# Cross-attention of a perceiver block on one Trainium2 core: scores in three products of 64 rows, probabilities turned 64 rows at a time

## The chip, the cores and the metric

The kernel runs on one core of one Trainium2 chip. The metric is the device time of one execution in microseconds (us); the time before is the median of three executions, 1401.89 us (1398.45 to 1401.93). PE is TensorE, ACT is ScalarE, DVE is VectorE, POOL is GpSimd, SP is the queue that issues most of the DMAs. Everything is float32. A product is made of operands split in two parts, hi (rounded, type fp32r) and lo (the rest).

## The reference, cut to what matters

Three layers follow each other: cross-attention of 8 x 64 queries to 8 x 1601 context rows, a second attention with 16 heads of 64, and a mixture of experts. The change touches the first alone:

```python
x = x + xattn(layernorm(x), ctx_1024, Wq, bq, Wkv, bkv, Wproj, bproj)
# B=8 batches, N=64 queries, K=1601 context rows, D=512, H=16 heads of hd=32
q = (x @ Wq + bq)  ;  kv = (ctx @ Wkv + bkv)  ;  k, v = kv[0], kv[1]
attn = softmax(einsum('bhnd,bhkd->bhnk', q * hd**-0.5, k))
out = einsum('bhnk,bhkd->bhnd', attn, v) @ Wproj + bproj
```

## The kernel before

**Tiling.** The 1601 context rows of a batch are 13 tiles of 128 rows (the last has 65). They are worked in two chunks (`CHUNK`): chunk 0 has 7 tiles (896 keys), chunk 1 has 6 tiles (705 keys, 706 with padding). The 16 heads are 8 pairs; a pair's 2 x 64 queries fill 128 columns of `Qs_hi` and `Qs_lo`, in which the two heads stand block-diagonal, so 64 rows (2 heads x 32) carry the contraction. These 64 rows stand twice in the partitions. `Ks0` and `Ks1` hold the keys of chunk 0 and 1: the hi part in partitions 0 to 63, the lo part in 64 to 127. One matmul of 128 rows thus gives Q_hi times (K_hi + K_lo), a second one gives Q_lo times (K_hi + K_lo): four terms.

**Units and steps.** The main loop has a unit for every batch b and chunk c, 16 in all: seven batches in a hardware loop of two units each, then the last batch. A unit has nine steps (`STEPS`). Step i of a unit (functions `unit` of each engine) does on PE, in this order: `scores(i)` for pair i (L786), `turn_probs(i, 0)` and `turn_probs(i, 1)`, which transpose the probabilities of pair i-1 into two PSUM banks (L800), one or two pieces of keys or values for the chunk that comes next (`make_kv`, helper `three`, L151 to L153), a transpose of new context rows (`turn_ctx`, L694), and `outputs(i)`, the probabilities of pair i-1 times the values (L812). The last unit makes no keys or values.

**Pieces.** A chunk's keys and values come in 15 pieces (chunk 0) or 14 (chunk 1), spread over the steps of the unit before by `SLOTS`: one in step 0, two in most of the others. A key piece (K) covers four heads by 512, 384 or 322 context rows, 12 matmuls; a value piece (V) one tile of 128 rows, 12 matmuls of 512 columns. The pieces use two banks in turn: PE starts piece n when DVE is done with piece n-2 (L837); piece 5 of chunk 0 waits until pieces 0 to 4 are all done. In unit c = 1 the keys of chunk 0 are made: in steps 0 to 2 the four K pieces of 512 rows and the first V piece, in step 3 piece 5, later three K pieces and a fourth of 384 rows. In unit c = 0 the keys of chunk 1 are made, of 384 and 322 rows.

**The other engines.** In each step ACT copies the two turned banks to `PT` as hi part (`probs_hi`, L488 and L491), takes the exponential of pair i with its sum (L501), then makes the hi part of the pieces (`kv_hi`, L416 for keys, L420 for values) and of the turned context (L405). DVE takes the largest score of pair i (`largest`, L619), makes the lo part of `PT` (L628 and L632), of the pieces (`kv_lo`, L539 and L545) and of the context (L527), and adds up the output (L664). Each engine works its instructions strictly in that order. A K piece is two instructions on ACT and two on DVE, one for each pair of heads, 64 partitions each; DVE's wait for both of ACT's:

```python
ins = nc.scalar.activation(Ks[c][0:64, 2 * i + h, o:o + wide], acc[64 * h:64 * h + 64, 0:wide],
                           ACT.Identity, bias=bkc[:, 2 * i + h:2 * i + h + 1])
```

**Before the loop.** The first 15 pieces are made by themselves beside the layer norm of x and the queries (L716 to L780 on PE). `bkc`, the keys' bias, comes by one DMA of 2 KB in 4-byte elements.

**Later.** The second attention (from 1000 us) makes its scores in `score_banks` (L1494) with three products of 64 rows, two heads in turn, one in partitions 0 to 63 and one in 64 to 127, each in a PSUM bank of its own. The change leaves it as it is.

Of the kernel before, what the change touches and what calls it, by code (L numbers as in the profile page):

```python
# [24 lines left out]
def perceiver_kernel(nc, x_in, ctx_in, Wq, bq, Wkv, bkv, Wproj, bproj,  # L25
# [3 lines left out]
    P = 128  # L29
# [15 lines left out]
    HALF = [2 * -(-w // 4) for w in WIDE]  # L45
# [18 lines left out]
    with ExitStack() as whole:  # L64
# [107 lines left out]
        Ks0 = late("Ks0", [P, NP, WIDE[0]], FR)  # L172
# [19 lines left out]
        Ks1 = early("Ks1", [P, NP, WIDE[1]], FR)  # L192
# [11 lines left out]
        bkc = early("bkc", [64, NP])  # L204
# [3 lines left out]
        part_s = early("part_s", [P, BE, 2, NP])  # L208
        whole_s = early("whole_s", [P, BE, NP])
        factor = early("factor", [P, 2 * NP * B])  # L210
        factorT = early("factorT", [P, P])
        top7 = early("top7", [P, NP])
# [55 lines left out]
        def prob_groups(c):  # L268

            return (range(0, 4), range(4, CHUNK[c][1]))  # L270
# [36 lines left out]
        def program(block):  # L307
# [32 lines left out]
            def _(sp):  # L340
# [4 lines left out]
                sp.dma_start(bkc[:, :], bkv[0:D].rearrange("(j r) -> r j", r=64), allow_slow_non_contiguous=True).then_inc(sem("bk_in"), 16)  # L345
# [18 lines left out]
                def units(b):  # L364
# [7 lines left out]
                    sp.wait_ge(sem("s_made"), pairs_before(b, 1) + 4)  # L372
# [3 lines left out]
                    sp.wait_ge(sem("s_made"), pairs_before(b, 1) + NP)  # L376
# [24 lines left out]
            def _(act):  # L401
# [6 lines left out]
                def kv_hi(n, acc, c, piece):  # L408
                    kind, s, i = piece_of(c, piece)
                    t0, _ = SUBS[c][s]  # L410
                    o = (t0 - CHUNK[c][0]) * P
                    act.wait_ge(sem("kv_made"), n + 1)
                    if kind == "K":
                        _, wide = sub_cols(c, s)
# [23 lines left out]
                act.wait_ge(sem("bk_in"), 16)  # L438
# [39 lines left out]
                def unit(b, c, turn0, ctx, beside=None):  # L478
# [3 lines left out]
                    def probs_hi(i, q):  # L482
                        n = turn_of_probs(i, q, ctx)
                        acc = bank(P_BANKS[q])
                        tiles = prob_groups(c)[q]
                        full = [t for t in tiles if tile_rows(CHUNK[c][0] + t) == P]
                        act.wait_ge(sem("turned"), turn0 + n + 1)
                        ins = nc.scalar.copy(PT[:, full[0]:full[-1] + 1, 0, :],  # L488
                                             acc[:, 0:P * len(full)].rearrange("p (t r) -> p t r", r=P))
                        if len(full) < len(tiles):  # L490
                            ins = nc.scalar.copy(PT[0:TAIL, tiles[-1], 0, :],  # L491
                                                 acc[0:TAIL, P * len(full):P * len(tiles)])
                        ins.then_inc(sem("turn_hi"), 1)
# [29 lines left out]
            def _(dve):  # L523
# [6 lines left out]
                def kv_lo(n, acc, c, piece):  # L530
                    kind, s, i = piece_of(c, piece)
                    t0, _ = SUBS[c][s]
                    o = (t0 - CHUNK[c][0]) * P
                    dve.wait_ge(sem("kv_hi"), n + 1)
                    if kind == "K":
                        _, wide = sub_cols(c, s)
                        for h in range(2):
                            j = 2 * i + h
                            ins = nc.vector.scalar_tensor_tensor(  # L539
                                out=Ks[c][64:128, j, o:o + wide], in0=acc[64 * h:64 * h + 64, 0:wide],  # L540
                                scalar=bkc[:, j:j + 1], in1=f32(Ks[c][0:64, j, o:o + wide]),
                                op0=ALU.add, op1=ALU.subtract)
# [22 lines left out]
                dve.wait_ge(sem("bk_in"), 16)  # L565
# [47 lines left out]
                def unit(b, c, turn0, ctx, beside=None, begin=None, between=None):  # L613
# [3 lines left out]
                    def largest(i):  # L617
                        dve.wait_ge(sem("s_made"), pair0 + i + 1)
# [3 lines left out]
                    def probs_lo(i, q):  # L622
                        n = turn_of_probs(i, q, ctx)
                        acc = bank(P_BANKS[q])
                        tiles = prob_groups(c)[q]
# [1578 lines left out]
```

## Time and profile before

| | us |
|---|---|
| median of 3 runs | 1401.89 |
| the profiled execution, its own time | 1393.57 |
| its span in the profile | 1391.8 |
| before the main loop | 0 to 69 |
| a unit c = 0 (step 0 to step 0) | 182.4 to 238.4 |
| a unit c = 1 | 238.4 to 296.6 |
| the last unit | about 922 to 955 |
| seam, second attention, experts | 955 to the end |

The profile has a page (busy time of each engine, the chain of work that ended last, costliest groups of instructions) and views of the trace: who waited for whom, the timeline, groups by form, and busy time in chosen stretches. A duration given for a PE instruction contains its way through the engine and overlaps with the next; the distance between two starts is what it costs. In a timeline neighbours of one form are merged ("x7"); a row has the start, the length of the merged stretch, the engine, the line, the operation, and tiles written and read; forms are rows*columns of the stationary block, then rows x columns of what is streamed. PEld is the load of the stationary block.

### The profile page before, as it was taken

How to read it: one execution, taken by the hardware profiler on the slowest of the kernel's cores; microseconds unless marked ns; L12 is line 12 of the kernel's file. 1: busy time of each engine (PE TensorE's matmuls, PEld its weight loads, DVE VectorE, ACT ScalarE, POOL GpSimd, SP SyncE). 2: the span in 40 equal slices, each digit the busy share in tenths (PEclk: the TensorE clock that was granted, in tenths of full speed). 3: DMA queues.
4: the chain of work that ended last, by engine and by line, in shares of the span. 5: the costliest groups of instructions: out<-in, count | busy, mean ns of one | idle time of the engine just before them, and what ended most of it. 6: DMA issues, size and time to landing. Idle time of an engine off the chain costs nothing.

```text
span 1391.8 us, 22065 instructions
## 1 busy us (share of the span) xinstructions
PE 1325.6 (95%) x7439; PEld 1149.9 (83%) x7440; DVE 937.9 (67%) x1512; ACT 760.0 (55%) x1327; POOL 101.6 (7%) x84
## 2 busy tenths in 40 slices
PE   7999999999999999999999999987899699999997
PEld 5898988888889898888889989976677587877776
DVE  6566666666667666666666766758488856487884
ACT  5465555565555555555556554654332526477772
POOL 0000000000000000000000000044452120000002
PEclk9999999999999999999999999999899899999999
DMA  5211121011111112101111010472538457399993
GB/s 196 95 54 32 30 52 43 26 45 35 44 30 38 30 34 60 30 26 45 45 34 45 23 39 27 82 156 71 94 112 307 149 197 255 112 349 333 342 346 106
DMA packets 126852, 145.11 MB, mean 104 GB/s; under 512 B 64072, under 2 KB 67528, under 8 KB 126800
## 3 DMA queue, kind: packets, MB, share of 16 engines
q1 hardware_dynamic: 125536, 140.44, 32.6%
q0 software_dynamic: 1280, 4.20, 0.9%
q8 instruction: 22, 0.36, 0.1%
q14 instruction: 14, 0.11, 0.0%
HBM read 124.75 MB, written 19.86 MB: 104 GB/s over the span
## 4 chain that ended last, share of the span: by engine, by line
PE 71%; DVE 13%; issue 6%; DMA 4%; ACT 4%; SPq 1%; DVEq 0%; POOL 0%; ACTq 0%
PE ps_scores L151 12%; PE ps_scores L153 12%; PE ps_scores L152 12%; PE ps_out L819 6%; PE ps_turn L807 5%; PE ps_scores L796 5%; PE ps_turn L694 2%; DMA wu_raw<-in_L_ffn_W_dram 2%; PE ps_scores L2116 2%; PE ps_scores L2114 2%; PE ps_scores L2115 2%; DVE stat L619 2%; DVE Ks L539 2%; ACT wu_hi L1823 1%; DVE wu_lo L2005 1%
## 5 line engine op out<-in xcount | busy, mean ns | idle before, releaser
L539 DVE SCALAR_TENSOR_TENSOR Ks<-ps_scores,bkc,Ks 64x384 fp32r<-64x384 f32 (+2 forms) x254 | 160.6, 632 | 143.4 <-ACT Ks L416 140.8
L151 PE MATMUL ps_scores<-cT_hi,Wkv_hi 128*128 128x384 f32 (+2 forms) x504 | 181.9, 361 | 0.0
L501 ACT ACTIVATE Pr<-ps_scores,stat 128x705 f32<-128x705 f32 (+1 forms) x128 | 119.5, 934 | 110.0 <-DVE stat L619 110.0
L153 PE MATMUL ps_scores<-cT_hi,Wkv_lo 128*128 128x384 f32 (+2 forms) x504 | 172.9, 343 | 0.0
L152 PE MATMUL ps_scores<-cT_lo,Wkv_hi 128*128 128x384 f32 (+2 forms) x504 | 172.4, 342 | 0.0
L416 ACT ACTIVATE Ks<-ps_scores,bkc 64x384 fp32r<-64x384 f32 (+2 forms) x254 | 149.4, 588 | 39.1 <-PE ps_scores L153 35.5
L545 DVE TENSOR_TENSOR Vs<-ps_scores,Vs 128x512 fp32r<-128x512 f32 (+1 forms) x103 | 71.2, 691 | 147.0 <-ACT Vs L420 146.4
L151 PE MATMUL ps_scores<-Wkv_hi,cT_hi 128*128 128x512 f32 (+1 forms) x412 | 169.9, 412 | 0.0
L488 ACT CAST PT<-ps_turn 128x512 fp32r<-128x512 f32 (+2 forms) x256 | 110.2, 483 | 102.4 <-PE ps_turn L807 101.5
L153 PE MATMUL ps_scores<-Wkv_hi,cT_lo 128*128 128x512 f32 (+1 forms) x412 | 161.8, 393 | 0.0
L152 PE MATMUL ps_scores<-Wkv_lo,cT_hi 128*128 128x512 f32 (+1 forms) x412 | 161.1, 391 | 0.0
L819 PE MATMUL ps_out<-PT,Vs 128*128 128x256 f32 x832 | 123.2, 286 | 16.2 <-DVE PT L632 11.9
L2005 DVE TENSOR_TENSOR wu_lo<-wu_raw,wu_hi 128x2048 fp32r<-128x2048 f32 x56 | 126.5, 2287 | 15.8 <-ACT wu_hi L1823 15.7
L628 DVE TENSOR_TENSOR PT<-ps_turn,PT 128x512 fp32r<-128x512 f32 (+2 forms) x256 | 130.0, 550 | 10.3 <-ACT PT L488 9.4
L819 PEld LDWEIGHTS ps_out<-PT,Vs 128*128 128x128 f32 x832 | 113.6, 189 | 27.6 <-DVE PT L632 15.5
L420 ACT CAST Vs<-ps_scores 128x512 fp32r<-128x512 f32 (+1 forms) x103 | 60.4, 586 | 138.0 <-PE ps_scores L153 137.1
L619 DVE TENSOR_REDUCE stat<-ps_scores 128x1 f32<-128x705 f32 (+1 forms) x128 | 125.7, 983 | 3.4 <-DVE stats L670 3.3
L1823 ACT CAST wu_hi<-wu_raw 128x2048 fp32r<-128x2048 f32 x56 | 105.8, 1917 | 21.0 <-DMA wu_raw<-in_L_ffn_W_dram 21.0
L807 PE MATMUL ps_turn<-ident,Pr 128*128 128x128 f32 x832 | 112.7, 274 | 0.0
L807 PEld LDWEIGHTS ps_turn<-ident,Pr 128*128 128x128 f32 x832 | 98.5, 141 | 5.8
L153 PEld LDWEIGHTS ps_scores<-cT_hi,Wkv_lo 128*128 128x128 f32 x504 | 94.7, 188 | 5.2
L152 PEld LDWEIGHTS ps_scores<-cT_lo,Wkv_hi 128*128 128x128 f32 x504 | 95.1, 189 | 4.0
(383 smaller groups left out, 2466.8 us busy)
## 6 DMA issues: line engine op xcount, KB each, us to landing
wu_raw<-in_L_ffn_W_dram SPq DMA_DIRECT2D x64, 1024.0 KB, 7.4
raw<-in_ctx_dram SPq DMA_DIRECT2D x16, 768.0 KB, 4.6
raw<-in_ctx_dram SPq DMA_DIRECT2D x8, 1024.0 KB, 5.4
raw<-in_ctx_dram SPq DMA_DIRECT2D x8, 512.0 KB
sorted_x<-zeros SPq DMA_DIRECT2D x1, 4096.0 KB, 14.9
sorted_out<-zeros SPq DMA_DIRECT2D x1, 4096.0 KB, 25.4
o_heads<-U SPq DMA_DIRECT2D x56, 64.0 KB, 1.7
oA<-o_heads SPq DMA_DIRECT2D x8, 448.0 KB, 9.4
```

The costliest lines, as they stand in the source:

```text
L151: nc.tensor.matmul(out_ap, sh, mh, start=(i == 0), stop=False)
L152: nc.tensor.matmul(out_ap, sh, ml, start=False, stop=False)
L153: last = nc.tensor.matmul(out_ap, sl, mh, start=False, stop=(i == len(pairs) - 1))
L416: ins = nc.scalar.activation(Ks[c][0:64, 2 * i + h, o:o + wide], acc[64 * h:64 * h + 64, 0:wide], ACT.Identity, bias=bkc[:, 2 * i + h:2 * ...
L501: nc.scalar.activation(Pr[:, i % 2, 0:VALID[c]], S_cols(c, 0, VALID[c], 0 if ctx else i % 2), ACT.Exp, bias=stat[:, 0, c, i:i + 1], accum_ ...
L539: ins = nc.vector.scalar_tensor_tensor(out=Ks[c][64:128, j, o:o + wide], in0=acc[64 * h:64 * h + 64, 0:wide], scalar=bkc[:, j:j + 1], in1= ...
L619: nc.vector.tensor_reduce(stat[:, 0, c, i:i + 1], S_cols(c, 0, VALID[c], 0 if ctx else i % 2), AX.X, ALU.max, negate=True).then_inc(sem("s ...
L628: ins = nc.vector.tensor_tensor(PT[:, full[0]:full[-1] + 1, 1, :], acc[:, 0:P * len(full)].rearrange("p (t r) -> p t r", r=P), f32(PT[:, f ...
L807: ins = nc.tensor.matmul(bank(P_BANKS[q])[0:M, at:at + P], Pr[:, (i - 1) % 2, t * P:t * P + M], ident[:, :], is_transpose=True, start=True ...
L819: ins = nc.tensor.matmul(psO_heads, Vs[c][0:M, t, i - 1, :], PT[0:M, t, :, :].rearrange("p a r -> p (a r)"), start=(t == 0), stop=(t == CH ...
L1823: nc.scalar.copy(wu_hi[v][:, :, :], wu_raw[v % RING][:, :, :]).then_inc(sem("wu_hi_done"), 1)
L2005: nc.vector.tensor_tensor(wu_lo[v][:, :, :], wu_raw[v % RING][:, :, :], f32(wu_hi[v][:, :, :]), ALU.subtract).then_inc(sem("wu_lo_done"), 1)
```

## The change

The scores become the three products Q_hi K_hi, Q_hi K_lo and Q_lo K_hi of 64 rows each. The keys of a chunk are cut in two halves (`HALF`: 448 and 448 in chunk 0, 384 and 322 in chunk 1). The first half stands, hi and lo, in partitions 0 to 63, the second in 64 to 127; `Ks` keeps its size. The six matmuls alternate between the two halves of the partitions and between two PSUM banks. A K piece of 512 rows (context rows 0 to 511 of chunk 0) straddles the cut at 448, so ACT and DVE each write it with four instructions (2 x 448 and 2 x 64 columns) in place of two; all other K pieces lie in one half. `bkc` is needed in both halves and comes by two DMAs. The probabilities are turned one head at a time: for each tile two transposes of 64 rows and 64 streamed columns, head 0 into one bank and head 1 into the other; both banks are told of after the last tile. ACT and DVE each copy two banks of 64 columns by 7 or 6 tiles, where chunk 1 had three instructions. The wait for the banks moves ahead of the scores. Some small buffers share memory.

```diff
-    HALF = [2 * -(-w // 4) for w in WIDE]
+    HALF = [448, 3 * P]
...
-        Ks0 = late("Ks0", [P, NP, WIDE[0]], FR)
+        Ks0 = late("Ks0", [P, NP, 2, HALF[0]], FR)
...
+        def key_halves(c, s):
+            o, wide = (SUBS[c][s][0] - CHUNK[c][0]) * P, sub_cols(c, s)[1]
+            found = []
+            for half, (h0, h1) in enumerate(((0, HALF[c]), (HALF[c], WIDE[c]))):
+                k0, k1 = max(o, h0), min(o + wide, h1)
+                if k0 < k1:
+                    found.append((half, slice(k0 - o, k1 - o), slice(k0 - h0, k1 - h0)))
+            return found
+        def turned_probs(c, h):
+            n = CHUNK[c][1]
+            return bank(P_BANKS[h])[:, 0:S * n].rearrange("p (t r) -> p t r", r=S)
+        def kept_probs(c, h, part):
+            return PT[:, 0:CHUNK[c][1], part, S * h:S * (h + 1)]
...
-                sp.dma_start(bkc[:, :], bkv[0:D].rearrange("(j r) -> r j", r=64), ...)
+                for half in range(2):
+                    sp.dma_start(bkc[64 * half:64 * half + 64, :], bkv[0:D].rearrange("(j r) -> r j", r=64), ...)
...
# kv_hi on ACT; kv_lo on DVE is cut in the same way
-                        for h in range(2):
-                            ins = nc.scalar.activation(Ks[c][0:64, 2 * i + h, o:o + wide], acc[64 * h:64 * h + 64, 0:wide],
-                                                       ACT.Identity, bias=bkc[:, 2 * i + h:2 * i + h + 1])
+                        for half, cols, to in key_halves(c, s):
+                            rows = slice(64 * half, 64 * half + 64)
+                            for h in range(2):
+                                j = 2 * i + h
+                                ins = nc.scalar.activation(Ks[c][rows, j, 0, to], acc[64 * h:64 * h + 64, cols],
+                                                           ACT.Identity, bias=bkc[rows, j:j + 1])
...
# probs_hi on ACT; probs_lo on DVE in the same way
-                        ins = nc.scalar.copy(PT[:, full[0]:full[-1] + 1, 0, :], ...)
-                        if len(full) < len(tiles):
-                            ins = nc.scalar.copy(PT[0:TAIL, tiles[-1], 0, :], ...)
-                        ins.then_inc(sem("turn_hi"), 1)
+                        nc.scalar.copy(kept_probs(c, q, 0), turned_probs(c, q)).then_inc(sem("turn_hi"), 1)
...
# scores on PE
-                        for part, Q in enumerate((Qs_hi, Qs_lo)):
-                            for k0, k1 in ((0, HALF[c]), (HALF[c], WIDE[c])):
-                                ins = nc.tensor.matmul(S_cols(c, k0, k1, 0 if ctx else i % 2), Q[:, i, :],
-                                                       Ks[c][:, i, k0:k1], start=(part == 0), stop=(part == 1))
-                        ins.then_inc(sem("s_made"), 1)
+                        if ctx and i >= 1:
+                            pe.wait_ge(sem("turn_lo"), turn0 + turns_free(i))
+                        for n, (part, Q) in enumerate(((0, Qs_hi), (1, Qs_hi), (0, Qs_lo))):
+                            for half, (k0, k1) in enumerate(((0, HALF[c]), (HALF[c], WIDE[c]))):
+                                rows = slice(64 * half, 64 * half + 64)
+                                ins = nc.tensor.matmul(S_cols(c, k0, k1, 0 if ctx else i % 2), Q[rows, i, :],
+                                                       Ks[c][rows, i, part, 0:k1 - k0], start=(n == 0), stop=(n == 2))
+                                if n == 2:
+                                    ins.then_inc(sem("s_made"), 1)
...
# turn_probs on PE
-                            ins = nc.tensor.matmul(bank(P_BANKS[q])[0:M, at:at + P],
-                                                   Pr[:, (i - 1) % 2, t * P:t * P + M], ident[:, :],
-                                                   is_transpose=True, start=True, stop=True)
-                        ins.then_inc(sem("turned"), 1)
+                            for h in range(2):
+                                rows = slice(64 * h, 64 * h + 64)
+                                ins = nc.tensor.matmul(bank(P_BANKS[h])[0:M, S * t:S * (t + 1)],
+                                                       Pr[rows, (i - 1) % 2, t * P:t * P + M], ident[rows, rows],
+                                                       is_transpose=True, start=True, stop=True)
+                                if t == last:
+                                    ins.then_inc(sem("turned"), 1)
```

## Rows read from the trace of the kernel before

**Rows 1.** The page: busy time of PE; engines' shares of the last chain.
```profile
PE 1325.6 (95%) x7439; PEld 1149.9 (83%) x7440; DVE 937.9 (67%) x1512; ACT 760.0 (55%) x1327; POOL 101.6 (7%) x84
PE 71%; DVE 13%; issue 6%; DMA 4%; ACT 4%; SPq 1%; DVEq 0%; POOL 0%; ACTq 0%
```

**Rows 2.** Busy time by stretch: one unit c = 0, one unit c = 1.
```profile
182.40:238.40 56.00, 54.91 (x342) 49.74 (x341) 37.89 (x64) 33.24 (x64) 0.00 (x0) 1.00 0.18 52
238.40:296.60 58.20, 57.88 (x334) 51.53 (x333) 37.34 (x71) 31.68 (x71) 0.00 (x0) 1.00 0.10 25
```

**Rows 3.** Who waited for whom, 68 to 922: us, times, longest; PE's own waits.
```profile
PEld ps_scores L796 <- ACT Pr L501: 5.6, 7, 0.9
PEld ps_out L819 <- DVE PT L628: 5.3, 8, 0.8
```

**Rows 4.** Timeline of PE, one step of a unit c = 0, then c = 1.
```profile
307.67 0.57 PE L796 MATMUL ps_scores<-Ks,Qs_hi 128*128 128x448 f32 x2
...
308.49 0.93 PE L807 MATMUL ps_turn<-ident,Pr 128*128 128x128 f32 x7
309.17 0.42 PE L151 MATMUL ps_scores<-cT_hi,Wkv_hi 128*128 128x384 f32 x1
309.43 0.33 PE L152 MATMUL ps_scores<-cT_lo,Wkv_hi 128*128 128x384 f32 x1
...
364.21 0.49 PE L796 MATMUL ps_scores<-Ks,Qs_hi 128*128 128x354 f32 x2
...
364.87 0.82 PE L807 MATMUL ps_turn<-ident,Pr 128*128 128x128 f32 x6
```

**Rows 5.** Timeline of PE, second attention: into and out of its 64-row scores.
```profile
1005.51 0.39 PE L153 MATMUL ps_scores<-x2T_hi,sW_lo 128*128 128x512 f32 x1
1005.83 0.39 PE L1494 MATMUL ps_turn<-QT_hi,KT_hi 64*128 64x256 f32 x2
1006.05 0.28 PE L1494 MATMUL ps_turn<-QT_lo,KT_hi 64*128 64x256 f32 x2
1006.16 0.28 PE L1494 MATMUL ps_turn<-QT_hi,KT_lo 64*128 64x256 f32 x2
...
1012.91 0.31 PE L1494 MATMUL ps_scores<-QT_hi,KT_lo 64*128 64x256 f32 x2
1013.15 0.50 PE L151 MATMUL ps_turn<-x2T_hi,sW_hi 128*128 128x512 f32 x1
1013.48 0.39 PE L152 MATMUL ps_turn<-x2T_lo,sW_hi 128*128 128x512 f32 x1
```

**Rows 6.** Timeline, four float32 transposes of 8 rows and 8 streamed columns.
```profile
1105.99 0.32 PEld L2074 LDWEIGHTS ps_turn<-ident,lgT 8*128 8x128 f32 x4 [1.02 <-ACT lgT L1801]
1105.99 0.41 PE L2074 MATMUL ps_turn<-ident,lgT 8*128 8x8 f32 x4 [0.83 <-ACT lgT L1801]
```

**Rows 7.** Groups by form, 68 to 922: the keys' hi and lo parts.
```profile
L539 DVE SCALAR_TENSOR_TENSOR Ks<-ps_scores,bkc,Ks 64x384 fp32r<-64x384 f32 x120 | 73.9, 616 | 66.8 <-ACT Ks L416 65.6
L416 ACT ACTIVATE Ks<-ps_scores,bkc 64x384 fp32r<-64x384 f32 x120 | 69.0, 575 | 13.3 <-PE ps_scores L153 12.5
L539 DVE SCALAR_TENSOR_TENSOR Ks<-ps_scores,bkc,Ks 64x512 fp32r<-64x512 f32 x56 | 42.0, 749 | 42.6 <-ACT Ks L416 42.2
L416 ACT ACTIVATE Ks<-ps_scores,bkc 64x512 fp32r<-64x512 f32 x56 | 38.2, 682 | 9.3 <-PE ps_scores L153 9.0
```

**Rows 8.** Timeline, a unit c = 1: pieces 3 and 4 leave, piece 5 starts.
```profile
370.16 1.51 DVE L539 SCALAR_TENSOR_TENSOR Ks<-ps_scores,bkc,Ks 64x512 fp32r<-64x512 f32 x2 [1.29 <-ACT Ks L416]
...
372.19 0.69 DVE L545 TENSOR_TENSOR Vs<-ps_scores,Vs 128x512 fp32r<-128x512 f32 x1
...
373.32 0.47 PE L151 MATMUL ps_scores<-Wkv_hi,cT_hi 128*128 128x512 f32 x1
```

**Rows 9.** Timeline: x turned before the loop; the outputs of the last unit.
```profile
30.88 1.10 PE L735 MATMUL ps_turn<-ident,x_tok 128*128 128x128 f32 x8 [2.91 <-DVE x_tok L137]
...
939.86 0.39 PE L819 MATMUL ps_out<-PT,Vs 128*128 128x256 f32 x1 [0.93 <-DVE PT L632]
```

More of the change, by code:

```diff
@@ L191, in perceiver_kernel @@
         early = area(EARLY, LATE)
-        Ks1 = early("Ks1", [P, NP, WIDE[1]], FR)
+        Ks1 = early("Ks1", [P, NP, 2, HALF[1]], FR)
         Vs1 = early("Vs1", [P, CHUNK[1][1], NP, P], FR)
@@ L203, in perceiver_kernel @@
                 early("rt1", [P, TT]), early("rs1", [P, TT]))
-        bkc = early("bkc", [64, NP])
+        bkc = early("bkc", [P, NP])
         bqc = early("bqc", [P, KC])
@@ L207, in perceiver_kernel @@
         part_f = early("part_f", [P, BE, 2, NP])
[L208 to L209 removed]
+        whole_s = top
         factor = early("factor", [P, 2 * NP * B])
         factorT = early("factorT", [P, P])
+        part_s = factorT[:, 0:BE * 2 * NP].rearrange("p (b c j) -> p b c j", b=BE, c=2)
         top7 = early("top7", [P, NP])
@@ L344, in _ @@
                     sp.dma_start(Wkv_raw[:, k, :], wkv[:, k, :]).then_inc(sem(f"wkv_in{k}"), 16)
-                sp.dma_start(bkc[:, :], bkv[0:D].rearrange("(j r) -> r j", r=64), allow_slow_non_contiguous=True).then_inc(sem("bk_in"), 16)
+                for half in range(2):
+                    sp.dma_start(bkc[64 * half:64 * half + 64, :], bkv[0:D].rearrange("(j r) -> r j", r=64),
+                                 allow_slow_non_contiguous=True).then_inc(sem("bk_in"), 16)
                 sp.dma_start(x_tok[:, :, :], x_rows).then_inc(sem("x_in"), 16)
@@ L532, in kv_lo @@
                     t0, _ = SUBS[c][s]
-                    o = (t0 - CHUNK[c][0]) * P
                     dve.wait_ge(sem("kv_hi"), n + 1)
                     if kind == "K":
[L536 to L542, printed above, removed]
+                        for half, cols, to in key_halves(c, s):
+                            rows = slice(64 * half, 64 * half + 64)
+                            for h in range(2):
+                                j = 2 * i + h
+                                ins = nc.vector.scalar_tensor_tensor(
+                                    out=Ks[c][rows, j, 1, to], in0=acc[64 * h:64 * h + 64, cols],
+                                    scalar=bkc[rows, j:j + 1], in1=f32(Ks[c][rows, j, 0, to]),
+                                    op0=ALU.add, op1=ALU.subtract)
                     else:
@@ new lines, in turns_free, with turn_probs @@
+                    def turns_free(i):
+                        return 0 if i == 1 else turn_of_probs(i - 1, 1, ctx) + 1
+                    def turn_probs(i):
+                        if not ctx or i == NP:
+                            pe.wait_ge(sem("p_exp"), pair0 + i + 1)
+                            pe.wait_ge(sem("turn_lo"), turn0 + turns_free(i))
+                            pe.sem_inc(sem("turn_begun"), 1)
+                        last = CHUNK[c][1] - 1
+                        for t in range(last + 1):
+                            M = tile_rows(CHUNK[c][0] + t)
+                            for h in range(2):
+                                rows = slice(64 * h, 64 * h + 64)
[4 more added lines that the diff above has]
+                                    ins.then_inc(sem("turned"), 1)
```

44 lines of the change are left out of this document (9 added, 35 removed).

## The prediction

> **What bounds the kernel now.** I read the page first: PE is busy for 95% of the span and makes 71% of the chain that ended last; DVE at 67% and ACT at 55% have room on the average [rows 1]. The change lies almost wholly in the main loop, so next the busy time by stretch: in a unit c = 0 PE is busy 54.9 of 56.0 us, in a unit c = 1 57.9 of 58.2 [rows 2]. Then the list of waits over the loop: PE's own are 5.6 us for the exponential and 5.3 us for the turned probabilities in 854 us, some 0.7 us in 7 and 8 places [rows 3]. So PE's stream of starts sets the loop, and a tenth of a microsecond in a step counts 120 times (8 steps, 15 units). But DVE's averages hide one tight place, which the timeline shows: in a unit c = 1 the value piece 5 starts on PE at 373.32, and what it waits for, piece 4 on DVE, ends at 372.19 + 0.69 = 372.88 [rows 8]. That is 0.44 us of slack, with DVE having stood idle for 1.29 us before piece 3 only because ACT was not done with it. Last, the second attention, since it already has pairs of 64-row products [rows 5].
>
> **The scores.** Before: four matmuls of 448 columns from 307.67 to 308.49, 0.82 us or 0.205 each; in c = 1 364.21 to 364.87, 0.66 us, 0.164 each [rows 4]. Do two 64-row matmuls on different halves run side by side? In the second attention each merged row is two of them ("x2"), and pairs of 256 columns start 0.11 to 0.12 us apart, 1006.05 to 1006.16 [rows 5]: two for what one of 256 columns costs by the slope of the rows above (0.205 to 0.164 for 94 columns, so about 0.12). They do. So the scores take three pair times: 3 x 0.205 = 0.615 in c = 0 (saves 0.205); in c = 1 the wider half decides, 384 columns, at the pitch of a 384-column matmul, 0.174 (0.164 for 354, and the same slope), 3 x 0.174 = 0.52 (saves 0.13).
>
> **The turns.** Before: seven transposes; to the second key matmul after them it is 308.49 to 309.43, and in steady state one takes 0.109 (0.68 for 6 of them and 0.03 of the last, whose rest hides behind the next load) [rows 4]. What binds one, its load or its 128 streamed columns? Four small transposes of the experts' routing have the same kind of transpose with the same 128-column block and only 8 streamed columns: four loads in 0.32 us, one of 0.136 and three pitches of 0.06; four transposes in 0.41, pitches near 0.065 [rows 6]. So the load costs 0.06 and it is the stream that takes 0.109, 0.85 ns a column. With 64 columns in each half side by side the stream needs 0.055 and the load 0.06: I take 0.062 for a pair. Seven pairs: 0.43 for 0.76, saves 0.33; six: saves 0.28. Bounds: 0.055 (the stream alone) and 0.124 (the two loads one after the other). ACT and DVE get both banks 0.43 us after the first transpose where they got the first bank after 4 x 0.109 = 0.44: nothing moves for them. Their copies cost the same in c = 0 and under 0.1 us less in c = 1 (three instructions become two).
>
> **Going in and out.** The pieces and the outputs stay at 128 rows, so each step goes from 128 to 64 rows and back. Into them: L153 starts at 1005.51 and lasts 0.23 (512 columns at 0.44 ns and the overhead in the rows of L796), so 1005.74 would be next; it is 1005.83, and the second pair comes 0.22 later instead of 0.12 [rows 5]. Together 0.19: the engine runs empty first, then the first load (0.11) stands bare. Out: the last pair starts at 1012.91, without a change the second matmul of 512 columns would be at 1012.91 + 0.12 + 0.23 = 1013.26, it is 1013.48: 0.22 [rows 5]. After a transpose a part of this is paid already (the first key matmul lasts 309.17 to 309.43, 0.26 for 0.17 [rows 4]), the pair is shorter, and I come to 0.20. The list of places is the same in all 15 units with pieces: 9 steps, each in and out. Bounds 0.15 and 0.23 a way; nothing below, since both crossings in rows 5 pay.
>
> The Trainium skill says the same of this ("TensorEngine Tiling (Array Packing)", Key Properties: changing the tiling mode drains the engine) and gives no price; the trace's price is the one used. A rule that speaks against the narrow transposes is in "TensorE: Matmul & The Clock Gate", LDWEIGHTS: a load takes its columns / 1.2 ns, so 107 ns for 128 columns however few rows. For the fp32r loads of rows 5 this holds (0.11); for the float32 transposes of rows 6 it does not (0.06). By it the turns would gain nothing; that result is the second rival.
>
> **Sum on PE.** A step in c = 0: +0.19 - 0.205 - 0.33 + 0.20 = -0.15. In c = 1: +0.19 - 0.13 - 0.28 + 0.20 = -0.02. A unit c = 0 has six such steps that count (1 to 5 and 7). Step 0 (scores alone) ends in the wait for the exponential and step 6 (one piece) in the one for the turned probabilities [rows 3]: both chains start at the scores, which come as early as before (+0.19 - 0.205), so nothing is won there. Step 8 (turns alone): in, with a cheap load, +0.15, -0.33, +0.20, zero. Unit: -0.9. The added wait ahead of the scores is for what outputs(i-1) had already waited for: nothing.
>
> **The keys' copies.** A K piece of 512 rows gets four instructions on each engine. ACT: 682 and 575 ns for 512 and 384 columns [rows 7] is 0.84 ns a column, so 629 for 448 and, as an estimate, 308 for 64: +0.255 a head pair, +0.51 a piece. DVE: 749 and 616, 1.04 a column, 682 and 284: +0.43. DVE waits for ACT, so 0.94 us in series. (Bounds: nothing, if 64 columns cost what 64 more cost; 0.94 is from a line through three widths down to 322.) Unit c = 1 has four such pieces ahead of piece 5. I follow the two queues through steps 1 to 3. Piece 0: +0.94 on DVE. Behind it stands the largest score of step 1, which ACT's exponential waits for, and behind that piece 1 on ACT: +1.9 when DVE is done with it. Piece 2's ACT part runs in ACT's free time: +2.0. Then largest, exponential, piece 3: +2.9, and piece 4 behind it: +2.9 at 372.88. With 0.44 of slack, piece 5 starts 2.45 late, whatever PE saved until then. Behind it come value pieces (one instruction each), and the queues recover. Step 0's crossings (+0.19 - 0.13 + 0.19) put piece 0 itself some 0.2 later, and steps 4 to 8 come out even (four of -0.02, and step 8 with +0.15 - 0.28 + 0.20): +2.6 a unit. This is why I expect a loss: seven units c = 1, and the four long pieces are all of the same chunk.
>
> **Before the loop.** The same pieces 0 to 3 stand in DVE's queue ahead of the layer norm, and PE stands 2.91 us idle for x at 30.88 [rows 9]. Going through the queues as above, pieces 0 to 2 bring +1.3 and piece 3, inside the norm, +0.43: +1.75. The second DMA for `bkc` takes SP some 0.7 us more and delays x_tok by as much; the wait in rows 9 is for DVE and not for that DMA, so it is hidden. **Last unit:** it is a chain of outputs, turns, ACT, DVE (PE waits 0.93 for DVE [rows 9]); ACT's and DVE's shorter copies bring about 0.1 a step: -0.7.
>
> **Total.** 8 x (-0.9) + 7 x 2.6 + 1.75 - 0.7 = -7.2 + 18.2 + 1.05 = +12. The profiled execution took 1393.57 (its span 1391.8 and 1.8 around it), so 1405.6 there; the runs shown have a median 8.3 above it, and I move the median by the same 12: 1414.
>
> **Rivals.**
> First, the other side: the copies' extra instructions stay hidden. Place: piece 5 in c = 1; it decides at 0.44 us of added delay, against my 2.9. For it: 0.94 a piece rests on a line extended to 64 columns, and DVE is idle a third of the unit (37.3 busy of 58.2 [rows 2]). Against: the idle time stands where DVE waits for ACT, in the very series that grows. Then -7.2, units c = 1 about +0.2 each (step 0's +0.25 and the rest from above), -0.7 and little before the loop: -7, 1395; with crossings of 0.15, 1389. Chance 0.18.
> Second, the loads bind the turns: a pair takes 0.109 or more, as for an fp32r block. For: 64-row float32 loads on two halves are nowhere in the trace. Against: rows 6, and fp32r loads do pair in rows 5. Then 0.047 x 7 x 8 x 8 = +21 in c = 0; in c = 1 only steps 4 to 8 count, 0.047 x 6 x 5 x 7 = +10; the waits of rows 3 take up some 6. 1414 + 25 = 1439. Chance 0.16.
> Third, the halves do not run side by side with blocks of this kind: scores +0.6, turns +0.3 a step: some +90, 1500. Rows 5 speak against it; 0.02.
> Fourth, all my costs at their low ends together (crossings 0.15, the 64-column instructions half as dear): -6 and -9, near 1399 to 1405, no change. Chance 0.12.
>
> **Chances and range.** Forecast 0.52, so slower 0.52 + 0.16 + 0.02 = 0.70, within 0.3% (1397.7 to 1406.1, about what a measurement tells from no change) 0.12, faster 0.18. The forecast's own range is 1406 to 1428 (pair time 0.055 to 0.08, crossings to 0.23). To hold eight in ten it goes from the first rival's 1396 to the second's 1440.
>
> **What would show it.** Rows of L796's successor "x2" at 0.205 apart: scores in pairs. Starts of the transposes' pairs 0.06 apart, or 0.11 for the second rival. 0.19 and 0.20 more at the crossings. The group of the keys' lo part with a 64x64 form near 284 ns, ACT's near 308. A new wait of PE for DVE's value piece 4, some 2 us in each unit c = 1, which then lasts near 60.8 us, and units c = 0 near 55. If no such wait shows, the forecast is wrong and the first rival right.

## The result: 2.6% slower, where 0.9% was forecast

The changed kernel takes 1435.62 us (median, 1433.36 to 1437.84), the kernel before 1400.17 beside it: ratio 1.026, 95% interval 1.024 to 1.028. The forecast was 1414 with a range of 1396 to 1440. The sign and the range hold, but the loss is 35 us and not 12. The profiled execution took 1435.29, its span 1433.5.

The page of the kernel after, as [rows 1], and its line of instruction packets:
```profile
PE 1331.7 (93%) x8527; PEld 1121.7 (78%) x8528; DVE 949.0 (66%) x1512; ACT 777.1 (54%) x1327; POOL 101.6 (7%) x84
q8 instruction: 78, 1.28, 0.4%
PE 60%; DVE 17%; issue 10%; ACT 7%; DMA 5%; SPq 1%; POOL 0%; DVEq 0%; ACTq 0%
```
The same line of packets on the page of before:
```profile
q8 instruction: 22, 0.36, 0.1%
```
PE is busy only 6 us more, in a span 42 us longer. What grew are "issue" (6 to 10% of the last chain), ACT and DVE on that chain, and the instruction packets, 22 to 78. None of my terms was about the last. The share of "issue" misleads here: e1 below, without the gaps that follow, has 10% as well.

Busy time by stretch, after, as [rows 2]: the first unit c = 0, a unit c = 1, the unit c = 0 behind it (columns: stretch, length, PE, PEld, DVE, ACT and POOL busy, granted clock, DMA share, GB/s):
```profile
73.90:128.60 54.70, 53.76 (x414) 46.91 (x414) 37.30 (x62) 33.61 (x64) 0.00 (x0) 1.00 0.17 50
248.40:311.90 63.50, 58.38 (x397) 49.70 (x396) 39.69 (x74) 34.94 (x72) 0.00 (x0) 1.00 0.10 24
312.00:368.20 56.20, 55.26 (x414) 48.11 (x414) 36.71 (x61) 32.03 (x62) 0.00 (x0) 0.97 0.18 52
```
From start of scores to start of scores the units c = 1 take 63.2 to 63.6 us (before 58.2; one 64.9, the last 61.3), the units c = 0 54.8 (before 55.9), but four of them 56.3. The loop starts at 73.9 (before 68.9) and its last unit at 960.5 (before 921.7). From there to the end it is 2.9 us more. So 5.0 before the loop, 33.8 in it, 2.9 behind: 41.7, the difference of the spans. It is above that of the medians, 35.4, since the profiled execution of before (1393.57) lay 6.6 us under its median. The 2.9 behind can't be told from chance: kernels that leave that part as it is (before, e2, e8 to e11) need 470 to 478 us for it, after 473.

PE's own waits in the loop, after, as [rows 3] (us in total, times, longest):
```profile
PE ps_scores L151 <- DVE Vs L554: 12.5, 7, 1.8
PE ps_scores L799 <- issue: 12.1, 6, 2.2
PE ps_out L832 <- DVE PT L634: 11.5, 16, 1.0
PE ps_scores L151 <- DVE Ks L548: 3.3, 7, 0.5
```
Seven waits of 1.8 us are the forecast wait for value piece 4, one in each unit c = 1. The six waits for "issue" ahead of the scores, 2.2 us each, were not forecast. They stand where PE's loop over the batches turns. The timeline of PE there, between the last two units above:
```profile
308.88 0.87 PE L832 MATMUL ps_out<-PT,Vs 128*128 128x256 f32 x6
311.95 1.11 PE L799 MATMUL ps_scores<-Ks,Qs_hi 64*128 64x448 f32 x4 [2.20 <-issue]
312.86 0.58 PE L799 MATMUL ps_scores<-Ks,Qs_lo 64*128 64x448 f32 x2
313.37 0.69 PE L151 MATMUL ps_scores<-cT_hi,Wkv_hi 128*128 128x384 f32 x1
```
PE stands for 2.2 us with nothing to wait for, and when it starts again the clock is down. Two stretches from there:
```profile
311.80:315.20 3.40, 3.25 (x12) 2.67 (x13) 1.09 (x1) 0.57 (x1) 0.00 (x0) 0.50 0.50 86
315.20:318.60 3.40, 3.40 (x34) 3.09 (x33) 0.79 (x2) 2.50 (x7) 0.00 (x0) 1.00 0.80 302
```
The granted clock is 0.50 (1.2 GHz) in the first and 1.00 in the second, and 12 matmuls run in the first where 34 run in the second. So a gap can cost twice: its 2.2 us, and 1.5 us of half clock right behind it. The four units c = 0 of 56.3 us are these. The unit c = 1 of 64.9 has its half clock (509.7 to 513.1) not behind a gap but at the end of the wait for value piece 4 (509.8).

### The profile page after: what moved, and what is told of

Its sections match the earlier page's. It is cut to its first block, busy times and chain, and to the rows that moved or that the text cites. A ratio compares the mean times of both kernels' runs of the same rounds, so it can differ in the third digit from the quotient of the medians.

```text
span 1433.5 us, 24234 instructions
## 1 busy us (share of the span) xinstructions
PE 1331.7 (93%) x8527; PEld 1121.7 (78%) x8528; DVE 949.0 (66%) x1512; ACT 777.1 (54%) x1327; POOL 101.6 (7%) x84
## 4 chain that ended last, share of the span: by engine, by line
PE 60%; DVE 17%; issue 10%; ACT 7%; DMA 5%; SPq 1%; POOL 0%; DVEq 0%; ACTq 0%
PE ps_scores L151 12%; PE ps_scores L153 10%; PE ps_scores L152 10%; PE ps_out L832 5%; PE ps_scores L799 4%; ACT Ks L433 4%; DVE Ks L548 3%; PE ps_turn L819 2%; DVE stat L628 2%; DMA b1rows<-b_parts 2%; PE ps_turn L694 2%; DVE wu_lo L2017 2%; PE ps_scores L2128 2%; PE ps_scores L2126 2%; PE ps_scores L2127 2%
## 5 line engine op out<-in xcount | busy, mean ns | idle before, releaser
L548 DVE SCALAR_TENSOR_TENSOR Ks<-ps_scores,bkc,Ks 64x384 fp32r<-64x384 f32 (+3 forms) x316 | 174.3, 552 | 161.7 <-ACT Ks L433 158.3
L151 PE MATMUL ps_scores<-cT_hi,Wkv_hi 128*128 128x384 f32 (+2 forms) x504 | 186.8, 371 | 3.3 <-DVE Ks L548 3.3
L433 ACT ACTIVATE Ks<-ps_scores,bkc 64x384 fp32r<-64x384 f32 (+3 forms) x316 | 165.3, 523 | 41.5 <-PE ps_scores L153 35.0
L502 ACT CAST PT<-ps_turn 128x448 fp32r<-128x448 f32 (+1 forms) x256 | 117.2, 510 | 89.7 <-PE ps_turn L819 89.3
L634 DVE TENSOR_TENSOR PT<-ps_turn,PT 128x448 fp32r<-128x448 f32 (+1 forms) x256 | 138.6, 583 | 12.1 <-ACT PT L502 10.1
L1835 ACT CAST wu_hi<-wu_raw 128x2048 fp32r<-128x2048 f32 x56 | 105.8, 1917 | 18.2 <-DMA wu_raw<-in_L_ffn_W_dram 16.4
L151 PEld LDWEIGHTS ps_scores<-cT_hi,Wkv_hi 128*128 128x128 f32 x504 | 96.3, 191 | 16.5 <-DVE Ks L548 4.2
L151 PEld LDWEIGHTS ps_scores<-Wkv_hi,cT_hi 128*128 128x128 f32 (+1 forms) x412 | 76.6, 186 | 31.7 <-DVE Vs L554 13.5
```

Of the source, the lines that this page charges most:

```text
L151: nc.tensor.matmul(out_ap, sh, mh, start=(i == 0), stop=False)
L433: ins = nc.scalar.activation(Ks[c][rows, j, 0, to], acc[64 * h:64 * h + 64, cols], ACT.Identity, bias=bkc[rows, j:j + 1])
L502: nc.scalar.copy(kept_probs(c, q, 0), turned_probs(c, q)).then_inc(sem("turn_hi"), 1)
L548: ins = nc.vector.scalar_tensor_tensor(out=Ks[c][rows, j, 1, to], in0=acc[64 * h:64 * h + 64, cols], scalar=bkc[rows, j:j + 1], in1=f32(Ks ...
L634: nc.vector.tensor_tensor(kept_probs(c, q, 1), turned_probs(c, q), f32(kept_probs(c, q, 0)), ALU.subtract).then_inc(sem("turn_lo"), 1)
L1835: nc.scalar.copy(wu_hi[v][:, :, :], wu_raw[v % RING][:, :, :]).then_inc(sem("wu_hi_done"), 1)
```

## The parts of the change measured by their own rows

Timeline of PE, one step of a unit c = 0, after, as [rows 4]:
```profile
83.78 0.28 PE L832 MATMUL ps_out<-PT,Vs 128*128 128x256 f32 x1
83.99 0.67 PE L799 MATMUL ps_scores<-Ks,Qs_hi 64*128 64x448 f32 x4
84.50 0.36 PE L799 MATMUL ps_scores<-Ks,Qs_lo 64*128 64x448 f32 x2
84.70 0.59 PE L819 MATMUL ps_turn<-ident,Pr 64*128 64x64 f32 x14
85.22 0.44 PE L151 MATMUL ps_scores<-cT_hi,Wkv_hi 128*128 128x384 f32 x1
85.50 0.34 PE L152 MATMUL ps_scores<-cT_lo,Wkv_hi 128*128 128x384 f32 x1
```
The last score pair takes 84.50 to 84.70, 0.20 (forecast 0.205). The two before it take 0.51, so the first has 0.10 too much, and 83.78 to 83.99 is 0.21 where an output matmul's pitch is 0.12: into 64 rows costs 0.19 (forecast 0.19). Fourteen transposes and the way out take 0.52: six pitches of 0.061 (forecast 0.062) and 0.15; the rest of the way out is in the first key matmul, 85.22 to 85.50, 0.28 for 0.26 before. From the first score to the second key matmul it is 1.51 us and 0.09 of late arrival, before 1.76 [rows 4]: a step is 0.16 shorter, and 0.15 was forecast.

The keys' copies in the loop, after, as [rows 7]:
```profile
L548 DVE SCALAR_TENSOR_TENSOR Ks<-ps_scores,bkc,Ks 64x448 fp32r<-64x448 f32 x56 | 38.1, 680 | 53.8 <-ACT Ks L433 53.4
L433 ACT ACTIVATE Ks<-ps_scores,bkc 64x448 fp32r<-64x448 f32 x56 | 35.2, 629 | 7.9 <-PE ps_scores L153 7.4
L433 ACT ACTIVATE Ks<-ps_scores,bkc 64x64 fp32r<-64x64 f32 x56 | 17.2, 308 | 0.7
L548 DVE SCALAR_TENSOR_TENSOR Ks<-ps_scores,bkc,Ks 64x64 fp32r<-64x64 f32 x56 | 16.0, 286 | 0.8
```
629, 308, 680 and 286 ns: forecast 629, 308, 682 and 284. The line through three widths held down to 64 columns.

Timeline in a unit c = 1, after, as [rows 8]: pieces 3 and 4 leave, piece 5 starts:
```profile
268.83 1.98 DVE L548 SCALAR_TENSOR_TENSOR Ks<-ps_scores,bkc,Ks 64x448 fp32r<-64x448 f32 x4 [1.76 <-ACT Ks L433]
...
271.31 0.68 DVE L554 TENSOR_TENSOR Vs<-ps_scores,Vs 128x512 fp32r<-128x512 f32 x1
...
272.05 0.50 PE L151 MATMUL ps_scores<-Wkv_hi,cT_hi 128*128 128x512 f32 x1 [1.77 <-DVE Vs L554]
```
PE starts piece 5 as soon as DVE is done with piece 4, and has stood 1.77 us for it.

## Experiments: the loop's turn

Theory: the loop's body outgrew PE's instruction memory. One turn has 1467 recorded instructions before (672 matmuls, as many loads, 123 of the sequencer) and 1738 after (808, 808, 122). The expectations below name some bodies by sums that come out a few higher (1744, 1757, 1675, 1670, 1699, 1728); outside them the text gives what the traces hold. The records are not quite whole: of e2's 290 added instructions three a turn have none.

**e1: after with PE's loop written out.**
```
-                with pe.Fori(0, BE) as b:
+                for b in range(BE):
```


> The changed kernel with PE's loop over the batches written out (the other engines keep theirs). Theory A, the loop's turn: PE's loop body grew from 1467 to 1744 recorded instructions and no longer stays in its instruction store, so that at each of six turns PE stands 2.2 to 2.5 us for instructions and its clock then halves for 3.4 us in most of them. Written out, the body is fetched in a straight line: the gap before the scores of a new batch goes, 6 x 2.3 plus about 5 x 1.5 of half clock, so about 1435.6 - 21 = 1414, near the forecast. Rival B, the gap is the tail of the copies' longer queues on ACT and DVE: nothing changes there, 1432 to 1437. Rival C, that fetching itself costs more than is thought, in or out of a loop: slower than 1436.

1424.58 us (1422.28 to 1428.61), ratio to before 1.019 (1.017 to 1.022). The gaps are gone, with no wait of PE for "issue" left in the loop; units c = 0 take 55.3, units c = 1 61.3, but two of them 62.8. The turn was 11.0 of the 35.4 us. The rest is 10.6 us above my 1414. Its waits, and the half clock in one of the two longer units:
```profile
PE ps_scores L151 <- DVE Vs L554: 12.7, 7, 1.8
PE ps_out L832 <- DVE PT L634: 10.2, 15, 0.9
PE ps_scores L151 <- DVE Ks L548: 3.3, 7, 0.5
385.30:388.80 3.50, 3.50 (x11) 2.57 (x10) 1.05 (x3) 0.94 (x2) 0.00 (x0) 0.52 0.20 42
```
It stands 1 us behind the end of a 1.8 us wait for value piece 4, with no gap near: here too the copies' wait was followed by half clock, in two units of seven.

**e2: before with 290 semaphore increments more in a turn** (nobody waits for that semaphore; a body of 1754).
```
             for i, ((sh, sl), (mh, ml)) in enumerate(pairs):
+                for _ in range(pads[0] + (pads[1] if i == 0 else 0)):
+                    pe.sem_inc(sem("pad"), 1)
...
+                pads[:] = [2, 2]
                 with pe.Fori(0, BE) as b:
...
+                pads[:] = [0, 0]
```


> The kernel before, with 290 more PE instructions per turn of its loop, all increments of an unused semaphore among the key and value products (10 a piece, 29 pieces): a body of about 1757 with the old arithmetic. Theory A: instruction fetches go on through the loop (the kernel before has none between 188 and 891 us), a gap of 2.2 to 2.5 us at each of six turns and half clock behind it, 1400 + 14 to 22 = 1414 to 1422. Rival B (queues of the copies) and rival C' (the 64-row products bring the gap): no gap, 1400 to 1403, unless the increments themselves show between the matmuls.

1410.56 us (1408.98 to 1412.70), ratio 1.0085 (1.0064 to 1.0105), under the 1414 I expected at least. The gap is there at each turn, in a kernel with nothing of the change:
```profile
PE ps_scores L800 <- issue: 12.5, 6, 2.2
PE ps_out L823 <- DVE PT L632: 3.3, 8, 0.5
```
There are 77 instruction packets, and two units c = 0 of 56.7 and 56.8 us, half clock again. The others behind a gap last 55.3 where before has 55.9: ACT and DVE catch up while PE stands, which gives 0.6 us back (PE's seven waits for the exponential, 4.3 us in before, become one of 0.4). The unit of 56.8 by stretch:
```profile
186.40:243.20 56.80, 56.40 (x341) 51.35 (x342) 36.79 (x61) 31.98 (x62) 0.00 (x0) 0.97 0.17 51
```

**e8: before with its loop written out**, the control for e1 and e4.

> Before with TensorE's loop written out and nothing else changed, the control for the written-out loops. Theory A (the loop of before costs nothing at its turn, since its body stays in the instruction memory, and straight-line fetch costs nothing): 1399 to 1401, unit lengths as before, but as many instruction packets as the written-out after has. Rival (writing the loop out wins time of its own, so that what e1 and e4 gained was not the change's loss taken back): 1390 to 1396.

1398.94 us (1396.80 to 1401.42), ratio 0.9996 (0.9984 to 1.0008): a tie. It reads 54 packets and its units last 55.9 and 58.2 as before. So reading instructions in a straight line costs nothing that shows. What costs is the turn of a long body, with its packets.

**e9, e10, e11: where the bound lies.** As e2, with other counts:
```
-                pads[:] = [2, 2]
+                pads[:] = [1, 3]
```
This is e9 against e2; e10 has [2, 0] there, e11 [2, 1].

> Before with 203 always-granted semaphore increments among TensorE's key and value products of a turn (e2 had 290): a body of about 1670 recorded instructions, as e6's 1675. Theory A (the instruction memory holds a body up to a bound between 1675 and 1744, whatever the instructions are): no gap at the turn of the loop, unit lengths of before, about 22 instruction packets, 1399 to 1403. Rival (increments and matmuls count differently, or the place of the branch decides): gaps of 2.2 to 2.5 us at each turn, 1408 to 1413.

> The same with 232 increments, a body of about 1699: one look for the bound. A bound in the middle of 1675 and 1744 leaves open whether the gap is there; with it a turn takes 2.0 to 2.5 us more and about 77 instruction packets are read, without it about 22.

> The same with 261 increments, a body of about 1728: one look for the bound. With a bound near 1710, where seven blocks of 256 instructions less what the body wastes at its ends would lie, the gap is there.

e9, a body of 1667: 1399.57 us, ratio 1.001 (0.998 to 1.004), no gap, 23 packets, though one of its ten runs took 1413.83. e10, 1696: 1413.76, with a gap at four of the six turns. e11, 1725: 1415.47, a gap at all six. e10 and e11 ran once each. Two turns in e10, one with and one without the gap:
```profile
416.53 0.88 PE L823 MATMUL ps_out<-PT,Vs 128*128 128x256 f32 x6
420.03 0.68 PE L800 MATMUL ps_scores<-Ks,Qs_hi 128*128 128x448 f32 x2 [2.63 <-issue]
...
534.25 0.88 PE L823 MATMUL ps_out<-PT,Vs 128*128 128x256 f32 x6
534.96 0.58 PE L800 MATMUL ps_scores<-Ks,Qs_hi 128*128 128x448 f32 x2
```
So the bound is near 1700 recorded instructions and not sharp: in one and the same execution a body of 1696 turns with the gap and without it. Between 100 and 880 us the instruction packets are 5 in e9 (no gap), 41 in e10 (four gaps) and 59 in e11 (six): 9 for each gap.

The Trainium skill says ("Runtime: NRT & Kernel Launch", Instruction fetch mechanics) that PE's instruction memory holds 2048 instructions and is filled in blocks of 256, and that a taken branch to a target outside a window of two blocks stalls the engine until the block is fetched. The traces agree with the stall and show its price here, 2.2 to 2.6 us. They put the bound for a loop below 2048, near 1700 as far as records count. A window of two blocks they don't bear out: a body of 1467 turns without a gap. What the runs show is the stall, its packets, and that both hang on the number of instructions in the body; that a memory no longer holds the body is my reading of it, and no run counts what the memory holds.

## Experiments: the keys' copies

**e3: before with its 512-column key pieces copied as 448 and 64.**
```
-                        for h in range(2):
+                        for k0, k1 in ((0, 448), (448, 512)) if wide == 512 else ((0, wide),):
+                            for h in range(2):
...
```


> The kernel before, with only the copies of the 512-row key pieces cut at 448 columns, four instructions each on ACT and DVE. The forecast's term: 0.94 us more in series a piece, 2.45 a unit c = 1 after 0.44 of slack, 7 x 2.45 + 1.75 before the loop = +19, so 1419; a wait of PE for DVE of some 2.5 us at piece 5 in each of seven units. The forecast's first rival, copies hidden: 1400 to 1402 and no such wait.

1421.41 us (1419.66 to 1426.45), ratio 1.017 (1.014 to 1.020). The cut alone costs 21.6 us. Units c = 1 last 61.1 for 58.2, units c = 0 stay at 55.9, and the loop starts at 73.8 for 68.9. Its main wait is the one forecast for the change, 1.7 us where I said some 2.5; smaller ones for DVE, of 0.2 and 0.25 us, come ahead of it:
```profile
PE ps_scores L151 <- DVE Vs L547: 11.8, 7, 1.7
```

Before the loop the cut does more than delay. PE turns x, in before [rows 9], here in e3 and then in after, each with its stretch from 28 to 50 us:
```profile
33.26 1.97 PE L737 MATMUL ps_turn<-ident,x_tok 128*128 128x128 f32 x8 [4.26 <-DVE x_tok L137]
28.00:50.00 22.00, 17.74 (x82) 14.66 (x81) 14.95 (x29) 8.64 (x15) 0.00 (x0) 0.84 0.06 20
```
```profile
33.31 1.97 PE L735 MATMUL ps_turn<-ident,x_tok 128*128 128x128 f32 x8 [4.28 <-DVE x_tok L137]
28.00:50.00 22.00, 17.72 (x82) 14.64 (x81) 14.99 (x30) 8.64 (x15) 0.00 (x0) 0.84 0.07 19
```
The wait grew from 2.91 to 4.3 us, and behind it the granted clock is 0.84 in the mean of 22 us where before has 1.00: some 7 us at half clock, 3.5 lost. The eight transposes take 1.97 for 1.10. But the profile of before is a fortunate one. In e8, which is before up to the loop, the same stretch has
```profile
30.78 1.50 PE L735 MATMUL ps_turn<-ident,x_tok 128*128 128x128 f32 x8 [2.92 <-DVE x_tok L137]
28.00:50.00 22.00, 19.22 (x92) 16.15 (x93) 13.94 (x24) 7.53 (x15) 0.00 (x0) 0.92 0.10 30
```
a wait of the same length with a clock of 0.92 behind it, and the loop starts at 70.3. In e11 it is 0.84, again behind a wait of 2.91, and the start is 71.6. So the length of the wait alone does not set the clock, and kernels that are before up to the loop start it anywhere from 68.9 to 71.6. The second DMA for `bkc` has no part in this: e3 has only the one of before, and starts its loop as late as after.

**e4: e1 with the cut pieces copied head by head**, and DVE told after the first head, so that it copies head 0 while ACT copies head 1.
```
-                        for half, cols, to in key_halves(c, s):
-                            for h in range(2):
+                        for h in range(2):
+                            for half, cols, to in key_halves(c, s):
...
+                            if h == 0 and (c, s) == (0, 0):
+                                ins.then_inc(sem("k_part"), 1)
```


> The changed kernel with PE's loop written out and the cut key pieces copied one head after the other: ACT tells DVE after the first head (the other half of the bank's partitions), so that the series is 0.94 + 0.97 + 0.97 = 2.88 us, as in the kernel before (2.89), in place of 3.8. Theory A with the forecast's terms: the wait at piece 5 (7 x about 2) goes as well, 1414 - 7 x 2.5 - 1 = 1395 to 1398, below the kernel before. If the load of the engines and not the series made the wait, ACT and DVE still carry four instructions a piece and it stays: 1412 to 1414.

1401.49 us (1398.10 to 1405.18), ratio 1.002 (1.0004 to 1.0037), 3.5 us above the 1395 to 1398 I expected and not below before. Against e1 it is 23.1 us. The wait for piece 4 is gone, and a unit c = 1 lasts 58.4 us:
```profile
PE ps_out L843 <- DVE PT L644: 11.1, 16, 1.0
PE ps_scores L810 <- ACT Pr L512: 3.0, 7, 0.5
```
```profile
184.80:240.20 55.40, 53.93 (x413) 46.99 (x412) 37.76 (x64) 33.21 (x64) 0.00 (x0) 1.00 0.17 53
240.20:298.70 58.50, 58.05 (x399) 49.84 (x398) 38.63 (x72) 33.80 (x72) 0.00 (x0) 1.00 0.09 26
```
The instructions are all still there; only the series of ACT and DVE was cut. From the loop's start to that of the last unit it is 3.0 us shorter than before; what stands ahead of the loop is 2.7 longer.

**e12: e4 with PE's loop kept**, which completes the square of loop and copies.

> e4 with TensorE's loop kept as in after: only the order of the copies of the cut keys' pieces is changed against after. Theory A (the loop's turn and the copies are two separate losses that add up): e4's 1401.5 plus the 11.0 us that after lost against e1, 1410 to 1415; units with c=0 54.8 or 56.3 us, with c=1 60.4 to 60.7, gaps of 2.2 to 2.5 us at the turn. Rival (what is left of the copies' wait and the gap hide each other): 1403 to 1407. Other rival (the loss at the turn grows as nothing else holds TensorE): over 1418.

1410.30 us (1408.04 to 1412.83), ratio 1.008 (1.005 to 1.011). The turn costs 8.8 us here and 11.0 with the slow copies; the copies cost 23.1 with the loop written out and 25.3 with it kept. So the two losses add up, to within 2.2 us.

## Experiments: scores and turns apart, and the best version

**e5: the scores alone** (keys, scores and e4's order of copies of after, turns of before, loop kept).

> After's scores (three products of 64 rows for each half of the keys, the cut keys' pieces copied head by head with VectorE told after the first head), with the turns of before and TensorE's loop kept; its body would be about 1531 recorded instructions (before 1467, after 1744). Theory A (the score pairs save 0.15 us a step with 448 and 448 keys and less with 384, and the two crossings between whole-array and 64-row matmuls cost 0.19 and 0.20 us once a step, whoever of the two parts brings them): a unit with c=0 +1.1 us and with c=1 +1.7 us against before, 20 us in the loop, +2.7 us before it: 1417 to 1424. Where a body of 1531 no longer stays in TensorE's instruction memory (gaps of over 2 us at the turn of the loop), 10 to 14 us more: 1428 to 1437. Rival (the scores carry the whole gain of the change and the crossings are hidden): at or under 1403.

**e6: the turns alone** (before with the turns and the probabilities' copies of after).

> After's turns (64-row transposes, one head each, side by side) with the scores, the keys and their copies of before, and TensorE's loop kept; its body would be about 1675 recorded instructions. Theory A (the pairs of transposes save about what the two crossings cost): +0.02 us a step with c=0, +0.07 with c=1: 1402 to 1407 if the body stays in the instruction memory, and with gaps of over 2 us at the turn of the loop 1412 to 1421. Rival (the turns alone win and the scores lose): under 1397. If e5 (1531) has no gap and this one (1675) has, the bound lies between them.

e5: 1419.85 us (1417.42 to 1420.47), ratio 1.014 (1.012 to 1.016), as expected, without a gap and with 22 packets. Units c = 0 last 56.8 and c = 1 59.8, against 55.9 and 58.2. e6: 1405.92 us (1400.86 to 1417.51), ratio 1.006 (1.003 to 1.008); its profiled run took 1400.86, units of 56.0 and 58.5, no gap. Each part alone pays the crossings and loses, e6 2.7 of its 5.5 us by the longer units of its profiled run. Together they pay once and, as e4 shows, gain 0.6 us in a unit c = 0. e6 and e9, with bodies of 1674 and 1667, scatter by 17 and 18 us where e4 with ten runs too has 7. That a gap comes in some of their executions would explain it; neither profile is of such a run, so it is not shown.

**e7: e4 with the low part of key piece 3 behind the layer norm.**
```
-                norm_vector(dve, 1, x_tok, x_tok, lnt1, between=lambda: first_kv_lo(3))
+                norm_vector(dve, 1, x_tok, x_tok, lnt1)
+                first_kv_lo(3)
```


> e4 (after, TensorE's loop written out, cut keys' pieces copied head by head) with the low part of the fourth keys' piece behind the normalisation on VectorE and not in the middle of it. In the trace of e4 that copy (1.97 us) stands between the variance and the reciprocal, whose root is there at 27.36 us, and TensorE waits 4.3 us for x_tok. Theory: TensorE's wait falls to about 2.6 us but some of it comes back at the next product of values, which needs that copy: loop start 71.6 to between 70.5 and 71.2, time 1400 to 1401, ratio to before 0.999 to 1.001. Rival (what stands before the loop is set by VectorE's sum, not by its order): loop start stays 71.6, time 1401.5, the ratio of e4 (1.002).

1400.63 us (1397.85 to 1403.52), ratio 1.0004 (0.999 to 1.002). The loop starts at 70.1, earlier than I said: PE's wait fell by 1.8 us, about as expected, and nearly all of it stays won:
```profile
30.41 1.97 PE L747 MATMUL ps_turn<-ident,x_tok 128*128 128x128 f32 x8 [2.51 <-DVE x_tok L137]
```
The clock behind this shorter wait is 0.92 all the same. e7 ties with before. No version of the change was found that beats it.

## Why the prediction was wrong, by its steps

**What bounds the kernel, scores, turns, crossings:** right; a step is 0.16 us shorter where 0.15 was forecast. The sum over a unit c = 0 was not: 0.9 was forecast, and e1 and e4 are 0.6 shorter. The loss is in step 6, which I took as even. PE's wait for the turned probabilities there, in before and in e4:
```profile
338.87 1.10 PE L819 MATMUL ps_out<-PT,Vs 128*128 128x256 f32 x7 [0.40 <-DVE PT L628]
340.38 1.10 PE L843 MATMUL ps_out<-PT,Vs 128*128 128x256 f32 x7 [0.94 <-DVE PT L644]
```
From scores to scores this step takes 5.68 us in e4 (335.72 to 341.40) for 5.30 (334.51 to 339.81): DVE works without a pause there, and part of what PE saved in the steps before comes back as a longer wait for it. After's units are 1.1 shorter since the gap ahead of them gives 0.5 more, as it gives e2 0.6.

**The keys' copies:** right in place, order and nearly in size. +2.6 a unit c = 1 was forecast, e1 has +3.1 and e3, with no other part of the change, +2.9. Over seven units that is 2.0 to 3.5 us more than forecast, and half clock behind the wait adds 1.5 to 1.7 us in some units (one in after, two in e1). e4, with the same instructions, shows that the series of the two engines made the loss and not their load.

**Before the loop:** the term was mis-sized, +1.75 for 5.0. The queues' delay was about right: PE's wait for x grew by 1.4, and one of 0.7 for Wkv_lo came ahead of it. What I left out is the clock, up to 3.5 us lost at half clock behind the wait. e3 has the whole 4.9. Up to 2.7 of that is the luck of the profile of before, since e8 and e11 start the loop 1.4 and 2.7 later with nothing changed ahead of it. **Last unit:** the 0.7 forecast doesn't show. From its start to its last output it takes 38.2 us for 38.0, and 36.0 to 39.1 in kernels that leave it as it is.

**Total: the step that failed.** The sum had no term for PE's instructions as such. I counted matmuls by their time alone, and as pairs take less time than what they replace they looked like a saving. They are more instructions: six score matmuls for four and fourteen transposes for seven, each with its load, 271 more records in a turn. That took the body over a bound near 1700, with gaps of up to 2.2 us at six turns and half clock behind four of them. e1 (11.0 us less without the loop) and e2 (10.8 more with before's own work) show it from both sides. I had looked at every engine's time and at no queue of instructions, though the page of before has a line for it. This term is 11.0 of the 23.4 us by which the loss was above the forecast. Without it e1 still loses 24.8 us and not 12: the terms above came out too small, and half clock behind PE's waits had no term either.

**Rivals:** the second rival's 1439 is the nearest number, with a mechanism that the rows exclude: pairs of transposes take 0.061 and not 0.109. The first rival's copies were not hidden. Score pairs at 0.20 exclude the third, and costs at the forecast's own values the fourth. One slip without weight: by its own slope a 384-column pair takes 0.177 and not 0.174, 0.07 us a unit.

The account in the profiled loop, 33.8 us: six units c = 1 longer than e1's by a gap of 1.9 to 2.3 us, 12.2; half clock behind four of the gaps, 6.0; half clock behind one wait for value piece 4, 1.7; seven units c = 1 of +3.1, 21.5; eight units c = 0, -7.6, of which about 3 are what the gaps give back. With 5.0 before the loop and 2.9 behind it that is 41.7. The forecast had nothing for the first three, 18.2 for the copies, -7.2 for the units c = 0, 1.75 before the loop and -0.7 behind.

## What to carry to other kernels

Count instructions as well as microseconds. Where a change splits matmuls inside a hardware loop, count one turn's instructions on PE before and after, and look at the instruction packets on the page: a loop that fits reads hardly any between its first and last turn. Where copies run in series over two engines, cutting one instruction in two doubles its overhead twice in that series; handing over after the first half takes it out again. And a stall of PE of 1.8 to 4 us can cost more than its length, since half clock may follow it. A saving on the busiest engine is not kept where the next one has no pause left: look at who waits for whom in each step, not over the unit.

## What the runs showed of the hardware beside this

- In the profiled executions PE's loop turned without a gap up to 1674 recorded instructions (e6), with one at four of six turns at 1696 (e10), and with one each time from 1725 on (e11, after, e12, e2).
- Half clock came behind some gaps and not others: behind four of six in after, four of four in e10, three of six in e12, two of six in e2, one of six in e11. Behind a wait of 1.7 to 1.8 us it came in one unit of seven in after, two in e1 and none in e3.
- 64-row float32 transposes of 64 columns take 0.061 us a pair where one of 128 rows and 128 columns takes 0.109, though each load of the pair is as many columns wide.
- Pairs of 64-row products of 448 columns take 0.20 us, what one 128-row product of the same width takes.
- A change between whole-array and 64-row work costs about 0.19 us in and 0.15 to 0.20 out, once for scores and turns together.
